# A graph layer on one core: three raw units of the router's early products moved into the second attention, and the second head's spread rows moved ahead of them

## What is computed

```python
xn = _layernorm(x)
x = x + graph_attention_layer(xn, edges) + linear_mixing(xn)    # 1250 nodes, 768 channels
x = x + expert_layer(_layernorm(x))                             # 8 experts, the 2 best of each token

# in the graph layer, twice: 4 heads of 192 channels, then 2 heads of 96
h = (x @ W).reshape(n, H, C)
s_src, s_dst = (h * a_src).sum(-1), (h * a_dst).sum(-1)
e = leaky_relu(s_src[src] + s_dst[dst], 0.2)
ee = exp(e - segment_max(e, dst)[dst])
out = segment_sum(ee / denom[dst] * h[src], dst) + bias         # then concat([x, out2]) @ Wu + bu
# in the expert layer
logits = flat @ router_w.T                                      # flat: the normalized rows
```

## Time and profile before

| | |
|---|---|
| median of 3 runs | 1091.47 us (1091.25 to 1094.06) |
| the profiled execution: its time | 1085.47 us |
| its span | 1083.7 us |
| TensorE busy | 947.0 us, 87% |
| VectorE busy | 667.2 us, 62% |
| ScalarE busy | 427.8 us, 39% |
| GpSimd busy | 386.6 us, 36% |
| mean granted TensorE clock | 0.933 |

### The profile page before, as it was taken

One profiled execution on the slowest core, in us unless ns is written; L12 is line 12 of the kernel. 1 busy time (PEld: TensorE's weight loads), 2 busy tenths in 40 slices (PEclk: granted clock), 3 DMA queues, 4 the chain that ended last, 5 costly groups with the idle time before them and its releaser, 6 DMA issues.

```text
span 1083.7 us, 14577 instructions
## 1 busy us (share of the span) xinstructions
PE 947.0 (87%) x5216; PEld 809.1 (75%) x5216; DVE 667.2 (62%) x1635; ACT 427.8 (39%) x689; POOL 386.6 (36%) x298
## 2 busy tenths in 40 slices
PE   3999996999999993994889998999679659999992
PEld 3898754776779993994888898989677358777771
DVE  7769998312761321665999886875897876133330
ACT  2544103233430000446667786643883523322220
POOL 3158888888888881001000000000000012433331
PEclk9999998899999996998899999996899859999997
DMA  9995556432353469014001100057007492656653
GB/s 294 231 204 111 124 120 177 69 44 0 65 112 43 88 178 277 2 26 141 1 1 50 34 31 1 2 197 251 16 1 250 170 351 59 122 118 125 134 105 58
DMA packets 77891, 118.73 MB, mean 110 GB/s; under 512 B 32545, under 2 KB 51547, under 8 KB 77821
## 3 DMA queue, kind: packets, MB, share of 16 engines
q0 software_dynamic: 35344, 40.37, 22.1%
q1 hardware_dynamic: 42477, 77.44, 22.1%
HBM read 85.42 MB, written 32.35 MB: 109 GB/s over the span
## 4 chain that ended last, share of the span: by engine, by line
PE 23%; DMA 18%; DVE 12%; issue 6%; ACT 3%; POOL 1%; SPq 0%; POOLq 0%; DVEq 0%; ACTq 0%
PE bank L1770 15%; DMA out<-yout,sb_negq 13%; PE bank L2008 6%; DVE pbuf L1466 5%; DVE pbuf L1454 4%; DMA cnt<-table 3%; PE bank L1781 1%; ACT vbuf L1025 1%; DMA early_d<-x 1%; ACT h L1011 1%; DVE sb_before L1374 1%; PE bank L2061 1%; DMA u_row<-m_d 1%; DMA xs<-early_d,sb_negq 1%; POOL cnt L707 1%
## 5 line engine op out<-in xcount | busy, mean ns | idle before, releaser
L691 POOL DMA_INDIRECT table<-match_n,slot_ix x168 | 279.9, 1666 | 92.8 <-issue 48.8
L2008 PE MATMUL bank<-h,pbuf 128*128 128x193 f32 (+1 forms) x1200 | 189.9, 318 | 38.8 <-DVE pbuf L1466 35.8
L2008 PEld LDWEIGHTS bank<-h,pbuf 128*128 128x128 f32 x1200 | 180.7, 195 | 47.7 <-DVE pbuf L1466 43.4
L1374 DVE CUSTOM_DVE_ANT_0 sb_before<-a_row,pen 128x1280 bf16<-128x1280 f32 x60 | 89.3, 1489 | 17.7 <-ACT pen L968 12.8
L1238 DVE SCALAR_TENSOR_TENSOR junk_k<-keyrow,key,sb_before 128x384 uint8<-128x384 f32 x168 | 93.0, 615 | 10.3 <-DMA keyrow<-key_d 9.1
L747 POOL DMA_INDIRECT xs<-early_d,sb_negq x7 | 7.4, 1058 | 250.5 <-DMA early_d<-x 244.6
L1770 PE MATMUL bank<-xnT_hi,w_hi 128*128 128x512 f32 (+1 forms) x216 | 85.4, 395 | 12.6 <-issue 9.0
L1034 ACT ACTIVATE pbuf<-pbuf 128x1280 f32<-128x1280 f32 x60 | 76.6, 1277 | 41.2 <-DVE pbuf L1454 41.2
L1466 DVE SCALAR_TENSOR_TENSOR pbuf<-pbuf,cnt 128x1280 f32<-128x1280 f32 x60 | 88.7, 1483 | 0.0
L1770 PE MATMUL bank<-w_hi,xnT_hi 128*128 128x384 f32 x240 | 83.9, 350 | 0.0
L771 POOL DMA_INDIRECT out<-yout,sb_negq x27 | 43.5, 1613 | 112.1 <-DMA out<-yout,sb_negq 84.3
(11 more groups left out here) (342 smaller groups left out, 1791.4 us busy)
## 6 DMA issues: line engine op xcount, KB each, us to landing
keyrow<-key_d SPq DMA_DIRECT2D x28, 384.0 KB, 3.7
cnt<-table POOLq DMA_DIRECT2D x20, 320.0 KB, 9.4
w_all<-in_w1T SPq DMA_DIRECT2D x8, 768.0 KB, 8.6
w_all<-in_w2T SPq DMA_DIRECT2D x8, 768.0 KB, 9.9
u_row<-m_d POOLq DMA_DIRECT2D x8, 640.0 KB, 6.0
w_raw<-in_kqvT SPq DMA_DIRECT2D x4, 1152.0 KB, 7.9
y_d<-x SPq DMA_DIRECT2D x10, 388.0 KB, 10.3
acc_d<-ubuf SPq DMA_DIRECT2D x20, 192.0 KB, 2.0
```

Source lines behind the costliest of these rows:

```text
L691: pool.indirect_dma_start(table[i], bass.IndirectOffsetOnAxis(ap=slot_ix[:, g:g + 1], axis=0), match_n[:, g:g + 1], None, compute_op=ALU.a ...
L1374: ins = nc.vector.tensor_tensor_reduce(out=junk_m[:, :], in0=rows_a[h][:, :], in1=pen_t[:, :], scale=1.0, scalar=-3e38, op0=ALU.subtract, ...
L2008: ins = nc.tensor.matmul(b[:, d * stride:d * stride + chans + 1], score[:, dt * P:(dt + 1) * P], h_t[:, st, h, 0:chans + 1], start=st == 0 ...
```

## The change

- Items 0 to 8 of `PRE` (`PRE_IN_MAX` = 9) stay in the stage of the masked maxima, in the same order. Head 1's spread rows follow item 8 at once.
- Items 9 (the last raw tile), 10 and 11 (the two weight tiles) go into the second attention. TensorE turns them behind units 0, 4 and 8 and multiplies them behind units 2, 6 and 10. ACT copies the turned items behind its exponentials of units 2, 6 and 10 and the products behind those of units 4, 8 and 12.
- The last raw tile has a fifth buffer, at 97600, and the late items are turned into `accb` and `row_t`. SP's load of tile 9 no longer waits until tile 5 has been turned; it waits for `pad_out`, a transfer issued during the first attention.
- The planner gives the three late items the banks 4, 5 and 6 past those of the attention's first head.

```diff
-        PRE_FIRST = 7
+        PRE_FIRST, PRE_IN_MAX = 7, 9
+        xa.append(at("xa_last", 97600, [P, D]))
+        xp += [v[:, :].rearrange("p (k t) -> p k t", k=KD) for v in (accb, row_t)]
...
         reserve_spread(1)
-        for h in range(H2):
-            for i in range(2):
-                reserve("agg2", h, i)
+        AGG2 = turn[0]
+        for i in range(2):
+            reserve("agg2", 0, i)
+        for i in range(PRE_IN_MAX, len(PRE)):
+            for k, name in enumerate((("preT", i, 0), ("preT", i, 1), ("pre", i))):
+                reserve(*name, at_bank=AGG2 + 4 + k)
+        for i in range(2):
+            reserve("agg2", 1, i)
...
             for t in range(NT):
-                if t >= XA:
+                if XA <= t < PRE_IN_MAX:
                     finished(sp, "preT", t - XA, 1)
-                sp.dma_start(xa[t % XA][:, :], acc_d[t * P:(t + 1) * P, :]).then_inc(xa_in[t % XA], 16)
+                if t == PRE_IN_MAX:
+                    sp.wait_ge(pad_out, 16)
+                sp.dma_start(raw_at(t)[:, :], acc_d[t * P:(t + 1) * P, :]).then_inc(raw_in(t), 16)
...
# ScalarE
                     for k in out_at.get(st, ()) if h else ():
                         bank_out(h - 1, k)
+                    if i in beside:
+                        beside[i]()
...
             spread_out(1)
             act.wait_ge(max_done, MAX1 + 2 * NT)
-            attention(H1, H2, u2_row_b, row_ready_2, {})
+            late = {}
+            for n, i in enumerate(range(PRE_IN_MAX, len(PRE))):
+                late[4 * n + 2] = lambda i=i: pre_turned(i)
+                late[4 * n + 4] = lambda i=i: pre_out(i)
+            attention(H1, H2, u2_row_b, row_ready_2, {}, late)
...
# TensorE
             pre_turned(0)
-            for i in range(len(PRE)):
-                if i + 1 < len(PRE):
+            for i in range(PRE_IN_MAX):
+                if i + 1 < PRE_IN_MAX:
                     pre_turned(i + 1)
                 pre_logits(i)
                 if i == PRE_FIRST - 1:
                     spread_rows(0)
             spread_rows(1)
-            aggregate("agg2", H1, H2, h2, S2, C2, 2, 5, {})
+            late = {}
+            for n, i in enumerate(range(PRE_IN_MAX, len(PRE))):
+                late[4 * n] = lambda i=i: pre_turned(i)
+                late[4 * n + 2] = lambda i=i: pre_logits(i)
+            aggregate("agg2", H1, H2, h2, S2, C2, 2, 5, late)
```

More of the change, by code:

```diff
@@ L194, in gps_layer, with raw_at, raw_in, turned_at @@
         PRE = [("x", t) for t in range(NT)] + [("w", j) for j in range(2)]
-        PRE_FIRST = 7
+        PRE_FIRST, PRE_IN_MAX = 7, 9
+        xa.append(at("xa_last", 97600, [P, D]))
+        xp += [v[:, :].rearrange("p (k t) -> p k t", k=KD) for v in (accb, row_t)]
+        def raw_at(t):
+            return xa[t % XA] if t < PRE_IN_MAX else xa[XA]
+        def raw_in(t):
+            return xa_in[t % XA if t < PRE_IN_MAX else XA]
+        def turned_at(i):
+            return xp[i % 2] if i < PRE_IN_MAX else xp[2 + i % 2]
         consts = wq[:, :, :].rearrange("p k f -> p (k f)")
@@ L294, in gps_layer @@
         g_in, g_hi_done, g_split = sem("g_in"), sem("g_hi_done"), sem("g_split")
-        xa_in = [sem(f"xa_in{i}") for i in range(XA)]
+        xa_in = [sem(f"xa_in{i}") for i in range(XA + 1)]
         centred, shift_done = sem("centred"), sem("shift_done")
@@ L1012, in bank_out, with attention @@
                 ins.then_inc(free("agg", h, i), 1)
-            def attention(h0, heads, u2_r, row_ready, out_at):
+            def attention(h0, heads, u2_r, row_ready, out_at, beside):
                 seq = [(h, st) for h in range(heads) for st in range(NT)]
@@ L1036, in attention @@
                         bank_out(h - 1, k)
-            attention(0, H1, u2_row, row_ready_1, {1: (0, 1), 2: (2, 3, 4)})
+                    if i in beside:
+                        beside[i]()
+            attention(0, H1, u2_row, row_ready_1, {1: (0, 1), 2: (2, 3, 4)}, {})
             act.wait_ge(g_in, 32)
@@ L1071, in pre_turned @@
                     w = P if PRE[i][0] == "x" else C2
-                    nc.scalar.activation(xp[i % 2][:, 3 * h:3 * h + 3, 0:w], b[:, 0:3 * w].rearrange("p (k t) -> p k t", k=3),
+                    nc.scalar.activation(turned_at(i)[:, 3 * h:3 * h + 3, 0:w], b[:, 0:3 * w].rearrange("p (k t) -> p k t", k=3),
                                          ACT.Copy).then_inc(free("preT", i, h), 1)
@@ L2054, in pre_turned @@
                 if kind == "x":
-                    pe.wait_ge(xa_in[t % XA], 16 * (t // XA + 1))
+                    pe.wait_ge(raw_in(t), 16 * (t // XA + 1) if t < PRE_IN_MAX else 16)
                 for h in range(2):
@@ L2060, in pre_turned @@
                         if kind == "x":
-                            ins = nc.tensor.transpose(b[:, j * P:(j + 1) * P], xa[t % XA][:, c], ident[:, :])
+                            ins = nc.tensor.transpose(b[:, j * P:(j + 1) * P], raw_at(t)[:, c], ident[:, :])
                         else:
@@ L2070, in pre_logits @@
                 for k in range(KD):
-                    ins = mm(b[0:n, 0:E], xp[i % 2][:, k, 0:n], rw_raw[:, k, :], k == 0, k == KD - 1)
+                    ins = mm(b[0:n, 0:E], turned_at(i)[:, k, 0:n], rw_raw[:, k, :], k == 0, k == KD - 1)
                 ins.then_inc(full("pre", i), 1)
```

## The result

The changed kernel took 1079.91 us in the median of 4 runs (1078.88 to 1084.0), against 1092.63 us of the kernel before: a ratio of 0.9896, 95% interval 0.986 to 0.9932. Two later comparisons with more runs gave 0.9945 (0.9915 to 0.9975) and 0.9939 (0.991 to 0.9968), 6 to 7 us.

A forecast was written before the change was run, and what follows sets the result against it. The prediction took TensorE's lateness for head 1's spread rows, behind three items not needed yet, as the bound. Its terms, -5.0 + 0.4 + 0.4 + 0.5 = -3.7 us, gave 1087.8 us, range 1085.2 to 1090.8 us.

The forecast's parts named there:

- What bounds the kernel, and what the change frees: Ahead of the second attention: TensorE, not DVE, is 5.04 us late for head 1's spread rows, kept by three items.
- the term of -5.0 us: Ahead of head 1's spread rows: without the three items they begin at about 747.2 instead of 752.17, 5.0 us sooner.
- TensorE is then idle for 3.8 us, and the spread rows take 7.37 us: At head 1's spread rows: TensorE waits 3.8 us for DVE's columns, then the rows take 7.37 us as before.
- The attention's price: In the second attention: the inserted items cost 0.4 + 0.4 us on TensorE and 0.5 us on ACT.
- the scores of unit 4: In the attention: item 9 turned behind unit 0 makes DVE wait, taken as 0.4 us.
- those of unit 6: In the attention: item 9 multiplied behind unit 2, not adding to the earlier delay; 0 us, at most 0.4.
- unit 10: In the attention: item 10 multiplied behind unit 6, 1.26 us of products, makes TensorE 0.4 us late.
- the change of heads: In the attention: ACT's copy of item 11 delays the exponential there from 795.00 to 795.5, 0.5 us.
- The clock in the attention: Past unit 2 of the second attention: no granted clock of 0.50 anywhere, else the prediction is wrong.
- The slower rival: Inserted narrow products keep the clock low in the attention; +8.9 us, 1100.4 us, from two low stretches on; chance 0.08.
- The queues, at nothing: SP's tile 9 load and five weight loads go out about 1.95 us sooner, nothing waits for them; costed at nothing.
- The sum: Whole kernel: -5.0 + 0.4 + 0.4 + 0.5 = -3.7 us, taken from the median, 1091.47 to 1087.8 us.

The follow-up runs named there:

- d4_mid: Against the changed kernel, TensorE turns item 9 in its idle time ahead of unit 0 instead of behind it; median 1084.62 us, ratio 0.987 to before.
- e2_wide_after: Changed kernel with the products of items 0 to 8 made 128 columns wide instead of 8; ratio 0.9943 to the kernel before.
- c4_load: Against the kernel before, only tile 9's own buffer and its load no longer waiting for tile 5, all twelve items left in the stage; ratio 1.0005.
- e1_wide_before: Kernel before with each item's six products 128 columns wide instead of 8, nothing moved; ratio 0.9884, median 1081.95 us.
- after: First profiled execution of the changed kernel; 1084.0 us.
- c1_before: The kernel before run again with no edit; ratio to itself 0.9989, median 1093.32 us.
- d3_behind: Against the changed kernel, items 9 to 11 turned and multiplied behind the whole second attention; ratio 0.9986 to before, median 1096.21 us.

## Why the prediction went wrong

- **What bounds the kernel, and what the change frees: right.** TensorE was late for head 1's columns because of items nobody needs yet, and the gain arrived at the start of the attention.
- **"An item is 1.95 us; TensorE is 5.04 us late", the term of -5.0 us: the step that failed.** Both numbers were right for the execution that was read the earlier trace rows, and not for the kernel. In it the items' first 10.85 us were at full clock. In two others of the same kernel 37.5 us of the stage were at half, an item at half was 3.73 us and TensorE 10.8 us late. The rows showed both falls of the clock behind 8-column products, and I used them for a rival in the attention, not for the stage itself, whose length hangs on them. Each item that runs at half adds 3.73 - 1.95 = 1.78 us, so the lateness had to be a range and not a fixed value. Measured: 49.8 to 56.3 us to the first scores before, 46.5 us after, 7.6 us on average instead of 5.0. The sum itself held a warning: it noted that the profiled execution was 6.0 us under the median, and still took that execution's stage off the median. The two others, at 1095.01 and 1094.14 us, had 6.5 us of the difference in this very stage.
- **"TensorE is then idle for 3.8 us, and the spread rows take 7.37 us": wrong twice, in my favour and against me, and right in sum by luck.** There was no idle in the three profiles of the changed kernel, since the remaining nine items, most of them at half clock, still ended 3.0 to 3.4 us late. But with only two items between them the two heads' spread rows stood 753.05 - 749.96 = 3.1 us apart, and head 1's fell into the full-clock stretch that began during head 0's (748.38 to 762.04): 4.71 us. So they ended 3.4 + 4.7 = 8.1 us behind DVE's last column, where 0.05 + 7.37 = 7.4 us were forecast. `d4_mid` (1.20 us idle and 7.58 us) and `e2_wide_after` (7.55 us and 7.36 us) show the other branch. The picture of after was thus nearly right in time; it was the kernel before whose time was taken too short.
- **The attention's price: mechanism right, size too large.** 0.83 us instead of 1.3: by the starts of DVE's instructions some 0.15 us at the scores of unit 4 (0.4 forecast), 0.33 us at those of unit 6 (0, in one with the former), 0.17 us at unit 10 (0.4), and 0.15 us at the change of heads (0.5), where the pair of products takes 3.06 us instead of 2.91. ACT's copy of item 11 took 0.68 us, not 0.87.
- **The clock in the attention: right.** It is 1.00 from 768.86 to 824, with the items in it. The slower rival did not come true there; its reason, that narrow products can cost the clock, held in the stage ahead.
- **The queues, at nothing: right within the 0.4% that `c4_load` can tell.**
- **The sum.** With the stage's means it would have been -7.6 + 0.8 = -6.8 us, 1084.7 us, just below the range; its lower end was built from one execution's clock. That would still have been 4.8 us above the 1079.91 us measured.

What stays open is the rest of the first comparison: 11.4 us where the stage gives 6.8. The part of the span behind the last two units of the attention varied between 262.0 and 267.4 us among the profiled executions that have nothing of the change in it (262.5 in before, 264.5 and 264.4 in its repeats, 262.0, 265.1 and 263.0 in the changed kernel), and the start of the stage between 709.1 and 719.1 us. That is enough to carry 4 to 5 us in medians of four runs, but it was not pinned down. The granted clock points the same way: the profiled run of the changed kernel had 0.926 and 1084.0 us, the other three of that comparison 0.933 and 1078.9 to 1080.4 us, and of its 24 later runs only 5 reached 0.933. But those 5 took 1081.7 to 1086.2 us, so the clock alone does not account for it. The exact moment of each fall is open as well: the same kernel had its stage at full clock for the first 15 us once and fell within 1.4 us of its start twice.

## What to carry to other kernels

Before costing moved TensorE work from one profile, see which clock it ran at, and read the same stage in a second execution: here a single stage of the unchanged kernel had lengths up to 6.5 us apart. Where the profiled execution is several us off the median, ask first whether the difference lies in the stage that is being priced. A stretch of narrow products on a fully busy TensorE can take longer than the same stretch with wide ones; look at the granted clock before moving such work, since making it wider may win more than hiding it. Work left ahead of a wait is not always waste: at full clock (`e1_wide_before`) the three items filled TensorE's wait, and taking them away (`e2_wide_after`) let the clock fall.

## What the runs showed of the hardware

- TensorE was at half clock for 23.9 us on end while it was busy for every one of them, for some 18 us of it on items of six transposes and six products of 8 columns (12 records), and then on spread rows (`after`, `c1_before`). With products of 128 columns and the same number of records the clock was 1.00 for 40.96 us (`e1_wide_before`). The wider records cost next to nothing: an item of 128 columns took 1.99 us at full clock, one of 8 columns 1.95 us at full clock and 3.73 us at half.
- Three items between units of an attention that left TensorE 0.62 us of room a unit cost 0.83 us in all; by themselves, behind the attention, they took 10.1 us (`d3_behind`).
- Six transposes, 0.88 us, in the middle of 6.3 us of idle time did not keep the clock up (`d4_mid`, one execution).
- In 35 runs of the kernel before, beside one another on one chip, the time went with the mean granted clock: 1088.4 to 1092.5 us where it was 0.931 to 0.933, and 1095.9 to 1103.6 us where it was 0.916 to 0.923.
